# Moving x2's centring, the row copies, the weight scaling and the last up products between engines in a gated cross-attention and FFN kernel

## The reference

```python
q = w8a8(layernorm(x), wq, bq); k = cond @ wk.T + bk; v = cond @ wv.T + bv
attn = softmax(q @ k.T / sqrt(32) + mask)                   # 16 heads
x = x + tanh(g_xattn) * w8a8(attn @ v, wo, bo)              # int8 rows, int8 weight rows
n = layernorm(x)
g = qlinear_fp8(n, w_gate); u = qlinear_fp8(n, w_up)        # rows gathered by an index
t = silu(g) * u
x = x + tanh(g_ffn) * qlinear_fp8(t, w_down)
```

## Time and profile before

| | us |
|---|---|
| median of 3 runs | 570.88 (569.48 to 573.16) |
| the profiled execution | 571.12 |
| its span, first to last instruction | 569.3 |
| mean granted TensorE clock, share of full | 0.955 |
| prologue (to the centring of x2 in step 2) | 136.15 |
| one steady step (193.97 to 250.05) | 56.08 |
| the six steps between the centrings, 136.15 to 477.26 | 341.1 |
| from there to the end | 92.0 |

### The profile page before, as it was taken

One profiled execution on the slowest core, in us unless ns is written; L12 is line 12 of the kernel. 1 busy time (PEld: TensorE's weight loads), 2 busy tenths in 40 slices (PEclk: granted clock), 3 DMA queues, 4 the chain that ended last, 5 costly groups with the idle time before them and its releaser, 6 DMA issues.

```text
span 569.3 us, 9874 instructions
## 1 busy us (share of the span) xinstructions
PE 449.5 (79%) x3030; PEld 272.7 (48%) x3030; DVE 487.7 (86%) x1254; ACT 461.4 (81%) x1129; POOL 232.8 (41%) x212
## 2 busy tenths in 40 slices
PE   0397496988998899889988988899889975963854
PEld 0274374555545554555455544554555443531321
DVE  5999789988798889888988798889888987699993
ACT  5779799998988798989888888898989886963350
POOL 4432262004653455246434642555246422541620
PEclk9999887999999999999999999999999998895967
DMA  8942352112114221322132113221321121000001
GB/s 259 387 139 79 98 149 56 38 57 38 56 27 94 62 57 26 89 68 57 27 104 52 57 26 84 74 55 27 91 65 20 27 53 30 20 0 16 20 17 74
DMA packets 61060, 39.51 MB, mean 69 GB/s; under 512 B 47568, under 2 KB 53712, under 8 KB 61008
## 3 DMA queue, kind: packets, MB, share of 16 engines
q1 hardware_dynamic: 56256, 27.47, 18.4%
q0 software_dynamic: 3328, 11.41, 6.3%
q10 hardware_dynamic: 1424, 0.01, 0.1%
HBM read 23.87 MB, written 4.19 MB: 49 GB/s over the span
## 4 chain that ended last, share of the span: by engine, by line
DVE 36%; POOL 14%; ACT 14%; issue 13%; PE 10%; DMA 5%; DVEq 0%; POOLq 0%; SPq 0%; ACTq 0%
POOL up L464 5%; POOL up L454 4%; DVE ts L1482 3%; ACT prob L655 3%; DVE q L1204 3%; POOL x L433 3%; DVE q_last L1305 3%; DVE prob L1305 2%; ACT q_last L655 2%; PE bank_h L887 2%; DVE rows L1421 2%; DVE t_sb L1199 2%; DVE stats L1411 2%; DMA t_sb<-in_L_ffn_w_up_dram,index 2%; ACT rows L571 2%
## 5 line engine op out<-in xcount | busy, mean ns | idle before, releaser
L454 POOL TENSOR_TENSOR up<-up,wgu_scale 128x512 f32<-128x512 f32 (+1 forms) x42 | 52.0, 1239 | 81.8 <-ACT up L635 81.8
L664 ACT ACTIVATE probT<-bank_h 128x512 f32<-128x512 f32 x128 | 68.5, 587 | 1.3 <-PE bank_h L887 0.7
L655 ACT ACTIVATE prob<-prob,neg_max 128x256 f32<-128x256 f32 x128 | 63.3, 498 | 5.5 <-DVE neg_max L1305 5.5
L655 ACT ACTIVATE q_last<-q_last,neg_max 128x256 f32<-128x256 f32 x128 | 63.5, 499 | 2.2 <-DVE neg_max L1305 2.1
L469 POOL TENSOR_TENSOR x<-x,y 128x512 f32<-128x512 f32 x14 | 19.9, 1423 | 101.6 <-DVE y L1495 101.6
L464 POOL TENSOR_TENSOR up<-gate,up 128x512 f32<-128x512 f32 (+1 forms) x42 | 59.5, 1423 | 3.7 <-DVE gate L1360 1.5
L1305 DVE CUSTOM_DVE_ANT_0 prob<-bank_h,mask_sb 128x256 f32<-128x256 f32 x128 | 47.4, 420 | 12.9 <-PE bank_h L828 12.9
L887 PE MATMUL bank_h<-ident,prob 128*128 128x128 f32 x256 | 39.9, 291 | 12.8 <-ACT prob L655 12.7
L1305 DVE CUSTOM_DVE_ANT_0 q_last<-bank_h,mask_sb 128x256 f32<-128x256 f32 x128 | 47.4, 417 | 0.0
L914 PE MATMUL bank_o<-probT,v_sb 128*32 128x256 f32 x512 | 36.0, 400 | 14.0 <-DVE v_sb L1233 8.0
L562 ACT ACTIVATE mag<-t_sb,ts 128x512 f32<-128x512 f32 (+1 forms) x42 | 28.6, 680 | 20.1 <-DVE ts L1487 12.6
(11 more groups left out here) (237 smaller groups left out, 1209.0 us busy)
## 6 DMA issues: line engine op xcount, KB each, us to landing
x_in<-in_x_dram SPq DMA_DIRECT2D x8, 512.0 KB, 3.6
c_in<-in_ctx_dram SPq DMA_DIRECT2D x8, 512.0 KB, 3.8
out_dram<-x POOLq DMA_DIRECT2D x7, 512.0 KB, 3.8
mask_sb<-in_mask_BxSxS_ff_dram SPq DMA_DIRECT2D x8, 256.0 KB, 3.0
t_sb<-in_L_ffn_w_down_dram SPq DMA_DIRECT2D x2, 704.0 KB, 5.5
t_sb<-in_L_ffn_w_down_dram POOLq DMA_DIRECT2D x2, 704.0 KB, 6.8
kf<-in_L_xattn_wq_dram SPq DMA_DIRECT2D x1, 1024.0 KB, 10.8
wkT<-in_L_xattn_wk_dram SPq DMA_DIRECT2D x1, 1024.0 KB, 13.5
```

Source lines behind the costliest of these rows:

```text
L454: pool.tensor_tensor(up[:, c % 2, 0:w], up[:, c % 2, 0:w], wu_scale[:, off:off + w], ALU.mult).then_inc(f["u_scaled"], 1)
L655: ins = act.activation(prob_of[slot4][:, t, :], prob_of[slot4][:, t, :], ACT.Exp, bias=neg_max[:, slot4, t:t + 1], scale=-1.0, accum_out=r ...
L664: act.activation(probT[:, (slot + 3) % 4, :, :].rearrange("p a b -> p (a b)"), HEAD_BANK[(slot + 3) % 4][:, :], ACT.Copy).then_inc(s["turn ...
```

## The change

- x2_centre moves from VectorE to ScalarE, as an Identity activation whose bias is the negative mean; x2_stats on VectorE also writes that negative mean and signals x2_neg_mean.
- sx_copy moves from VectorE to ScalarE.
- pro_q and pro_o (VectorE) become pro_copy_q and pro_copy_o on ScalarE.
- The scaling of the raw weight pairs, seven on ScalarE and four on VectorE, becomes unit_lift on GpSimd for all eleven. unit_round waits for it.
- For batch 7, gate_scale makes only the gate; ScalarE's up_copy and GpSimd's up_scale do the up chunks as for the other batches.
- New orders on all five engines in all four kinds of step. On SP the mask load of a steady step stands ahead of t_turn(0), and waits for 16 heads of the step before and this one to be masked, which head_mask(11) completes; in tail_order t_turn(2) is back in its place. On ScalarE o_int comes ahead of head_probT(0), x_int behind x2_centre, sx_copy behind head_exp(4), t_mag_2(13) and group_oT(13) ahead of head_exp(12). On TensorE head_turn(1) comes ahead of y_project. On VectorE the blocks keep their places but for small swaps; in tail_order batch 6's t_sum and t_sub of its second tile come ahead of batch 7's first gate_scale, and on TensorE its first down product ahead of batch 7's x2T_turn.

The core of the diff (of the orders, the parts that the text speaks of):

```diff
-        DVE_UNITS = (7, 9, 11, 13)
...
+        def pairs_to(k):
+            return sum(1 for j in range(k + 1) if UNITS[j][0] == "pair")
...
-                k.x_turn(0); k.x_turn(1); k.x_load(0); k.mask_load(0); k.ctx_load(0)
+                k.x_turn(0); k.x_turn(1); k.x_load(0); k.ctx_load(0); k.mask_load(0)
...
-                k.o_turn(0); k.o_turn(1); k.x_turn(0); k.x_turn(1); k.x2_turn(0); k.x2_turn(1); k.x_load(0); k.t_turn(0)
-                k.t_turn(1); k.t_turn(2); k.ctx_load(0); k.t_turn(3); k.t_turn(4); k.t_turn(5); k.mask_load(0)
+                k.o_turn(0); k.o_turn(1); k.x_turn(0); k.x_turn(1); k.x2_turn(0); k.x2_turn(1); k.x_load(0)
+                k.mask_load(0); k.t_turn(0); k.t_turn(1); k.t_turn(2); k.ctx_load(0); k.t_turn(3); k.t_turn(4)
+                k.t_turn(5)
...
+                def unit_lift(slot):
+                    for k in W and lifted_unit(SLOTS * b + slot) or []:
+                        if UNITS[k][0] == "pair":
+                            raw = unit_raw(k)
+                            pool.wait_ge(s["wf_mag"], k + 1)
+                            for n in range(2):
+                                ins = pool.tensor_scalar(raw[:, n * C:(n + 1) * C], raw[:, n * C:(n + 1) * C],
+                                                         wf_r[:, k % 3, 0, n:n + 1], None, ALU.mult)
+                            ins.then_inc(s["wf_lifted"], 1)
...
-                    if OLD:
-                        pool.wait_ge(f["u_scaled"], 6 * B2 + c + 1)
-                    else:
-                        pool.wait_ge(f["u_ready"], 1 + 6 * B2 + c + 1)
+                    pool.wait_ge(f["u_scaled"], 6 * B2 + c + 1)
...
-                k.load(6); k.x_var(0); k.load(4); k.load(8); k.load(10); k.x_plus_bias(4); k.load(14); k.load(12)
+                k.load(6); k.load(4); k.x_var(0); k.unit_lift(4); k.unit_lift(6); k.load(10); k.load(8); k.load(12)
+                k.x_plus_bias(4); k.unit_lift(12); k.load(14); k.unit_lift(14)
 
             def second_step_order(k):
-                k.load(2); k.x_plus_bias(4); k.load(0); k.load(4); k.x_var(0); k.load(8); k.load(6)
+                k.load(0); k.unit_lift(0); k.x_var(0); k.unit_lift(2); k.load(2); k.load(4); k.load(6); k.unit_lift(4)
+                k.unit_lift(6); k.load(8); k.x_plus_bias(4); k.unit_lift(8); k.unit_lift(10); k.unit_lift(12)
 
...
+                e.x2_var(2); e.up_scale(6); e.gate_up(6); e.up_scale(7); e.gate_up(7); e.up_scale(8); e.gate_up(8)
+                e.up_scale(9); e.gate_up(9); e.up_scale(10); e.gate_up(10); e.up_scale(11); e.gate_up(11); k.out_add(13)
+                k.out_add(15); k.out_store(16); e.out_store(16)
...
+            def pro_evac(name):
+                for e in pieces(name):
+                    piece = PRO[e][1]
+                    act.wait_ge(s["pro_turned"], e + 1)
+                    for o in range(2):
+                        col = (2 * piece + o) * P
+                        ins = act.activation((wqT if name == "q" else woT)[:, :, col:col + P],
+                                             half(pro_bank(e))[:, o * C:(o + 1) * C].rearrange("p (c o) -> p c o", c=CC), ACT.Copy)
+                    ins.then_inc(s["pro_out"], 1)
...
-                    for n in range(0 if k in DVE_UNITS else 2):
-                        ins = act.activation(raw[:, n * C:(n + 1) * C], raw[:, n * C:(n + 1) * C], ACT.Copy, scale=wf_r[:, k % 3, 0, n:n + 1])
...
+                def x2_centre(slot):
+                    act.wait_ge(f["x2_neg_mean"], d - 1)
+                    for t in range(NT):
+                        ins = act.activation(rows[:, t, :], x2[:, t, :], ACT.Identity,
+                                             bias=neg_mean2[:, 0 if f is s else 1, t:t + 1])
+                    ins.then_inc(f["x2_centred"], 1)
+
+                def sx_copy(slot):
+                    act.wait_ge(s["sx_ps"], b + 1)
+                    act.activation(sx_row[:, :], O_BANK[:, N:2 * N], ACT.Copy).then_inc(s["sx_ready"], 1)
...
+                k.o_int(0); k.head_probT(0); k.x_centre(0); k.head_exp(0); k.head_exp(1); k.k_out_0(3); k.x_round(2)
+                k.head_probT(1); k.head_exp(2); k.head_exp(3); k.group_oT(1); k.head_probT(2); k.head_probT(3)
+                k.head_probT(4); k.x2_centre(3); k.x_int(2); k.group_oT(5); k.x2_mag_0(3); k.x2_mag_1(3); k.head_exp(4)
+                k.sx_copy(7); k.head_exp(5); k.k_out_1(4); k.head_exp(6); k.up_copy(6); k.head_exp(7); k.gate_tanh(6)
+                k.up_copy(7); k.head_probT(5); k.head_probT(6); k.head_probT(7); k.head_probT(8); k.q_high(8)
...
-                k.head_probT(0); k.o_int(0); k.x_centre(0); k.head_exp(0); k.head_exp(1); k.k_out_0(3); k.x_round(2)
-                k.x_int(2); k.head_exp(2); k.head_exp(3); k.head_probT(1); k.head_probT(2); k.head_probT(3)
-                k.head_probT(4); k.group_oT(1); k.x2_mag_0(3); k.group_oT(5); k.x2_mag_1(3); k.head_exp(4)
-                k.head_exp(5); k.k_out_1(4); k.head_exp(6); k.up_copy(6); k.head_exp(7); k.head_probT(5); k.up_copy(7)
-                k.gate_tanh(6); k.head_probT(6); k.head_probT(7); k.head_probT(8); k.up_copy(8); k.gate_tanh(7)
...
+                k.t_mag_2(13); e.up_copy(6); e.up_copy(7); e.gate_tanh(6); e.up_copy(8); e.gate_tanh(7); e.gate_tanh(8)
+                e.up_copy(9); e.gate_tanh(9); e.up_copy(10); e.t_mag_0(10); e.t_mag_1(10); e.up_copy(11)
+                e.gate_tanh(10); e.t_mag_2(11); e.gate_tanh(11); e.t_mag_0(12); e.t_mag_1(12); e.t_mag_2(13)
...
-                if k in DVE_UNITS:
-                    for n in range(2):
-                        dve.tensor_scalar(raw[:, n * C:(n + 1) * C], raw[:, n * C:(n + 1) * C], wf_r[:, k % 3, 0, n:n + 1], None,
-                                          ALU.mult).then_inc(s["wf_lifted"], 1)
-                    dve.wait_ge(s["wf_lifted"], 2 * DVE_UNITS.index(k) + 2)
+                if UNITS[k][0] == "pair":
...
-                    if not OLD:
-                        dve.wait_ge(f["u_ps"], 1 + 6 * B2 + c + 1)
-                        dve.scalar_tensor_tensor(up[:, c % 2, 0:w], U_BANK[:, 0:w], x2s[:, 5, t:t + 1], wu_scale[:, off:off + w],
-                                                 ALU.mult, ALU.mult).then_inc(f["u_ready"], 1)
...
                     ins.then_inc(f["x2_moments"], 1)
-
-                def x2_centre(slot):
                     dve.wait_ge(f["x2_moments"], d - 1)
-                    for t in range(NT):
-                        ins = dve.tensor_scalar(rows[:, t, :], x2[:, t, :], mv2[:, t, 0:1], None, ALU.subtract)
-                    ins.then_inc(f["x2_centred"], 1)
+                    dve.tensor_scalar(neg_mean2[:, 0 if f is s else 1, :], mv2[:, :, 0], -1.0, None, ALU.mult).then_inc(f["x2_neg_mean"], 1)
...
+                e.x2_sub_1(4); k.t_sum_0(12); e.x2T_copy(5); k.t_sub_0(12); k.t_sum_1(12); k.t_sub_1(12); k.t_sum_2(13)
+                k.t_sub_2(13); e.gate_scale(6); e.gate_scale(7); e.t_mul(7); e.gate_scale(8); e.t_mul(8)
+                e.gate_scale(9); e.t_mul(9); e.t_scales(9); e.gate_scale(10); e.t_mul(10); e.gate_scale(11)
```

More of the change, by code:

```diff
@@ L24 @@
 SpBlocks = namedtuple('SpBlocks', """x_load ctx_load mask_load x_turn o_turn x2_turn t_turn""")
[L25 to L27 removed]
+PoolBlocks = namedtuple('PoolBlocks', """load unit_lift x_var x2_add x2_var x_plus_bias up_scale gate_up out_add out_store""")
+ActBlocks = namedtuple('ActBlocks', """pro_copy_q pro_copy_o pro_round_q unit_mag_0 gate_tanhs pro_round_o wo_scaled oqT_high k_out_1 x_int o_int tT_high up_copy t_mag_0 t_mag_1
+t_mag_2 head_exp head_probT group_oT o_round k_out_0 x_centre x_round x2_centre sx_copy x2_mag_0 x2_mag_1 q_high gate_tanh unit_copy
 unit_mag""")
```

242 lines of the change are left out of this document (110 added, 132 removed).

## The result

The changed kernel is slower. Its median is 578.92 us (577.07 to 580.83, four runs) against 571.36 for the kernel before; the ratio is 1.0137, with a 95% interval of 1.0106 to 1.0168. I had forecast 564.2 and a range up to 574.0. The profiled execution took 577.77, its span is 575.9: 6.6 more than the 569.3 of before.

A forecast was written before the change was run, and what follows sets the result against it. No engine was full: a steady batch was half VectorE's, half a latency chain; ScalarE bound the second prologue batch. Prologue -7.5, steady batches +3.3 and tail -2.5 gave -6.7 on the 570.9 median: 564.2 us, range 556 to 574.

The forecast's parts named there:

- Prologue, second batch: ScalarE bounds it: four pair scalings leave, one copy comes, -4.7 us; 0.8 given back for rounds waiting on lifts.
- The price: Each GpSimd lift in the prologue takes 0.8 us (0.4 to 1.24), 18 us in all, covered by GpSimd's waiting.
- Prologue, first batch: Turned gathers end a VectorE wait, -2.8 us, and unit 7's scaling leaves VectorE, -0.8; sum -3.6.
- That wait goes, -2.8: First prologue batch: gathering unit 8 before unit 9 removes VectorE's 2.77 us wait at 64.34.
- The swap of o_int: Steady batches: o_int ahead of head_probT(0) on ScalarE starts the scores 0.5 us later (bounds 0 to 1.1).
- The centring: Steady batches: moving x2's centring to ScalarE costs net 0.05 us a batch, 1.7 against 1.49 and 0.17.
- the -mean: VectorE's added write of the negative mean before the centring in steady batches takes 0.17 us.
- By ScalarE's new list it arrives within 0.1 to 0.3 us: Steady batches: ScalarE reaches x2_centre within 0.1 to 0.3 us of the -mean.
- swaps that add nothing: Steady orders: most swaps lie inside VectorE's full half and add no work.
- ScalarE late at the centring: Rival, chance 0.20: ScalarE reaches x2_centre 2 us behind the -mean in each steady batch, +13 us, 577.
- The rival with the GpSimd queue and the port: Rival, chance 0.22: 22 prologue lifts each cost 0.33 us more on the path, 7.3 us, time 571.5.
- Tail: -2.5 us: VectorE loses six up products and the last centring, GpSimd gets six products; bounds -5 and +2.

The follow-up runs named there:

- number 9: Changed kernel with each of the 22 unit_lift instructions on GpSimd covering only 256 of 512 columns: 577.6 us, ratio 1.0118 to the kernel before.
- number 8: Changed kernel with GpSimd's x_plus_bias of the first batch moved behind that batch's last unit_lift: 574.37 us, ratio 1.0058 to the kernel before.
- numbers 3 and 4: Kernel before with x2's centring alone on ScalarE (583.61 us), and the same with steady x_plus_bias also moved behind x2_var (588.33 us).
- numbers 5 to 7: Changed kernel with centring back on VectorE (581.9 us), with group_oT(5) behind x2_mag_0 again (581.02), and with both (577.96).
- number 3: Kernel before with x2's centring alone moved to ScalarE: 583.61 us, ratio 1.0221.
- number 2: Kernel before with GpSimd's steady x_plus_bias moved behind x2_var, waiting until the first half of x2 is quantised: 570.66 us, ratio 1.0004.

## Why the prediction was wrong

The sum was -7.5 + 3.3 - 2.5 = -6.7; the trace shows -0.1 + 8.1 - 1.4 = +6.6. Of the 13.3 between them 7.4 lie in the prologue, 4.8 in the steady batches and 1.1 in the tail.

**Prologue, second batch: right.** I took 4.7 off for ScalarE and gave back 0.8 for lifts, 3.9 in all. From the first mask to the last o_round the kernel won back 4.7 (from +4.6 to -0.1), and number 9 shows that the lifts cost next to nothing although each takes 1.56, above my upper bound of 1.24 (which was a mean over 512 and 384 columns; a product of 512 takes 1.27). The price was wrong, the cover right.

**Prologue, first batch: the step that failed, by 8 us.** "That wait goes, -2.8": the gather of unit 8 did come early, and nothing followed. Without the hold (number 8) the first masks begin at 54.60, 0.5 later than before. The path to them is q product, q_scale, v product, scores. The wait of 2.77 at 64.34 lay behind them and stood beside another chain; now VectorE waits 1.82 at 70.44 for a part of the v product instead. That part (66.77) takes 3.63, at a granted clock of 0.53 in its stretch, where the two parts of this size took 1.98 and 1.88 in the kernel before, and the next scores, which stand behind it on TensorE, start only at 73.23. From the first masks to the next batch's it is 15.9 us in both kernels. Which of the new orders lets the clock fall there is not tested. An idle of the engine is not a gain until one has seen that nothing else ends at the same time. On top came the hold of x_plus_bias, +4.0 with the slower v product behind it, which number 8 shows. I had weighed the order of the loads, but not what x_plus_bias, in its new place, would meet on VectorE.

**Steady batches: one step right, one wrong, one not priced.** The swap of o_int: predicted 0.5, measured 0.42 in a clean batch. The centring: "net 0.05 a batch", measured 0.8 on x2_max. The term that failed is the -mean, 0.96 and not 0.17. Behind it stand two more misreadings that are not paid on top of it here: of the 1.49 of the centring on VectorE only 0.88 was work, the rest was the hold that stayed behind; and ScalarE is not free when the mean is ready without a hold (numbers 3 and 4). "By ScalarE's new list it arrives within 0.1 to 0.3 us" was right only because the mean was late too (0.19). The new list also puts group_oT(5) ahead of x2_mag_0, which I had counted among swaps that add nothing; it alone holds x2_mag_0 at the same point (numbers 5 to 7). The last 0.34, from the second tile's reduction to o_round, is in VectorE's full half; 0.23 of it is idle time ahead of the first mask of the next batch at 404.53, which the profile puts down to issue; those scores end at 404.46. No run isolates it.

The rival that I gave 0.20, ScalarE late at the centring, named the right place. That its time (577) is close is luck: it added 13 us for a ScalarE 2 us behind the -mean, and in the changed kernel it is 0.1 to 0.2 behind; what is paid is 4.8 more than forecast, for other reasons, and the rest is the prologue's missing gain. The rival with the GpSimd queue and the port had the right cause, contention between VectorE and GpSimd, with the wrong parties: not the lifts but x_plus_bias holds, and not the wide rounds pay but two-column scales. The Trainium skill (SBUF — State Buffer, section Who interferes with whom) says it more fully than I had used it: besides two-input instructions, `copy`, `cast` and `tensor_scalar` can, where their operands allow it, enter modes that take the pair of ports shared with GpSimd; the side that issues first has it for the whole instruction, and the other blocks. The trace agrees that they are held (0.96 and 2.60 for two columns, 1.63 for 0.88), not that the recorded starts show who issued first (see the last section); read in full, it would have named the -mean as a victim.

**Tail.** I expected the last reduction 18 us behind GpSimd's first product and 22.9 to the end; it was 19.5 and 21.5. The first was 1.5 short, as t_mul is held by GpSimd's products there; the second is the clock.

**What stays open:** why the centring alone (number 3) makes the disturbed batches so long, and which of the new orders brings its steady batches from 355.7 together back to 348.2 (a part may be the slow execution that was profiled); which order lets the clock fall at the second part of the v product; and what lets the last down product run at full clock.

## What to carry to other kernels

Look at the spread of a line's instructions, not at one row: 473, 483 and 1235 ns for the same shape say that something holds it, and the hold stays in place when the work is moved away; it takes the next small instruction. Before counting an engine's idle time as room, look at what the engine does at the moment when its input is ready. Moving the instruction that holds is no cure either until one has looked at what it meets in its new place (number 2). When two waits end together, undoing one shows nothing, so test them together before calling either innocent.
